# Moving a quarter of the step computation of a graph-attention layer from VectorE to GpSimd

## The chip, the cores and the metric

The kernel runs on one core of one Trainium2 chip. Time is device microseconds of that core, from one launch. Below, PE is TensorE (matmuls), DVE is VectorE, ACT is ScalarE, POOL is GpSimd and SP is SyncE. Each engine runs its own list of instructions in order; the lists are tied together only by semaphores, which an instruction raises when it completes and which another engine's list waits for.

## The reference

Two layers over a graph of 4096 nodes with 512 features, each followed by a layer norm. The change lies in the first:

```python
wh = (x @ weight).reshape(n, 8, 64)
awh_i = (wh * linear_i).sum(axis=2)
awh_j = (wh * linear_j).sum(axis=2)
e = leaky_relu(awh_i[:, None, :] + awh_j[None, :, :], negative_slope=0.2)
e = e + ((1.0 - adj) * -1e10)[:, :, None]
a = softmax(e, axis=1)
out = einsum('ijh,jhf->ihf', a, wh)
x = layernorm(x + out)
```

The second layer is an 8-head dot-product attention with the same mask, and a second residual and layer norm.

A leaky ReLU inside an exponential splits by the sign of awh_i + awh_j: on either side of zero the exponential is a product of a factor of i and a factor of j. So the kernel needs, for every pair and head, only a bit that says whether the sum is positive. That bit is the "step" below.

## The kernel before

The kernel runs in stages, one after the other: the projection (`project_gat`), tables and the transposed adjacency (`build_tables`), the first attention (`gat`, lines 442 to 687), the projections of the second layer, its attention, and the end.

In `gat` the 4096 nodes i are taken in 8 chunks of 512, and each chunk in 8 heads: 64 units. In a unit the 4096 nodes j are 32 tiles of 128, taken four at a time, a quad: 8 quads in a unit, 512 in the stage. The buffers `step`, `pos` and `neg` have 4 slots each (`RING`), one quad in a slot. For each quad n:

- ScalarE makes three of the four step tiles (line 544): a very steep sigmoid of the row `arow` (awh_i for 512 nodes, the same in all partitions) with a per-partition bias, written as fp8, 0 or 1. It waits until `pos` of quad n-4 is made.
- VectorE makes the fourth tile, number 3 (`OWN`), in `own_step`, line 562: `arow + a_j > 0`, also fp8.
- VectorE makes `pos` (`positive`, line 575), the step's bytes and-ed with the edge's bytes `strip`, over all four tiles at once as 512 words of 32 bits; then `neg` (`negative`, line 582), `pos` xor `strip`. An edge's byte is fp8 2^-6, a single bit, and the step's 1.0 has that bit set.
- TensorE uses the 16 blocks of 128x128 bytes of `pos` and of `neg` as weights and streams 130 columns of the value table through each (line 677): 32 matmuls a quad, into `acc`.

VectorE's list is written out by hand: `positive(n)`, `own_step(n + 1)`, `negative(n)`, and so on, so the step of the next quad stands between the two. After the third quad of a unit it reads the accumulators of the unit before (`evacuate`, lines 589 to 595), and after the last head of a chunk it divides, adds the residual and takes the norm's statistics, in five pieces during the quads 2 to 6 of the next unit (lines 599 to 632). `positive(n)` waits for both step makers and for the matmuls of quad n-4; `negative(n)` waits for `positive(n)` to have completed.

GpSimd's list in this stage holds only the store of the chunk's result (line 686), once per chunk. SyncE loads the tables and rows; the next row of `arow` is loaded once both step makers have finished a unit.

Of the kernel before, what the change touches and what calls it, by code (L numbers as in the profile page):

```python
# [23 lines left out]
F32 = mybir.dt.float32  # L24
# [3 lines left out]
F16 = mybir.dt.float16  # L28
F8 = mybir.dt.float8e4
U32 = mybir.dt.uint32  # L30
ALU = mybir.AluOpType
ACT = mybir.ActivationFunctionType
X = mybir.AxisListType.X
# [2 lines left out]
P = 128  # L36
N = 4096
D = 512
H = 8
F = D // H  # L40
KB = D // P
NT = N // P
CW = 512
C = N // CW
TC = CW // P
U = C * H
# [209 lines left out]
def build_tables(nc, k, adj, scr):  # L256


    with ExitStack() as ctx:
        s = Space(nc, ctx, "b")  # L260
# [88 lines left out]
        @block.vector  # L349
        def _(dve):  # L350
            link = Chain(dve, chain)
            dve.sem_inc(row_out[0], 16)
            dve.sem_inc(row_out[1], 16)
            dve.sem_inc(t_done, 2)
            dve.wait_ge(loaded, 32)
            link(nc.vector.tensor_reduce(k.top_wh[:], tops[:, 0:P], X, ALU.max))
            link(nc.vector.tensor_scalar(k.top_wh[:], k.top_wh[:], 1e-30, None, ALU.max))
            link(nc.vector.reciprocal(inv[:], k.top_wh[:]))
            m_j = tops[:, P + H:P + 2 * H].unsqueeze(1).to_broadcast([P, NT, H])

            link(nc.vector.tensor_tensor(shift[:], k.a_j[:], m_j, ALU.subtract))

            link(nc.vector.tensor_tensor(t1[:], k.a_i[:], m_j, ALU.add))
            link(nc.vector.tensor_scalar(t2[:], t1[:], SLOPE, None, ALU.mult))
            link(nc.vector.tensor_tensor(k.row_factors[:, :, :, 0], t1[:], t2[:], ALU.max))
            link(nc.vector.tensor_tensor(t1[:], t1[:], k.row_factors[:, :, :, 0], ALU.subtract))
            link(nc.vector.tensor_tensor(t2[:], t2[:], k.row_factors[:, :, :, 0], ALU.subtract))
            nc.vector.tensor_scalar(k.steep[:], k.a_j[:].rearrange("p t h -> p h t"), STEEP, None, ALU.mult).then_inc(ready, 1)
            dve.wait_ge(exped, 4)
            link(nc.vector.tensor_scalar(vf[:], vf[:], VSCALE, None, ALU.mult))  # L370
            link(nc.vector.tensor_scalar(vg[:], vf[:], inv[:, 0:1], None, ALU.mult))
            link(nc.vector.tensor_copy(vh[:], vf[:]))
            link(nc.vector.tensor_tensor(vl[:], vf[:], vh[:], ALU.subtract))
            dve.sem_inc(ready, 1)
            for i in range(0, NT // 2):
                for b in range(4):
                    g = 4 * i + b
                    dve.wait_ge(adj_in[b], 16 * (i + 1))

                    dve.wait_ge(t_done, g + 1)  # L380
                    nc.vector.tensor_scalar(none[:, b % 2], stage[:, b], EDGE, None, ALU.mult).then_inc(cast, 1)  # L381
                    dve.wait_ge(row_out[b % 2], 16 * (2 * i + b // 2 + 1))
                    nc.vector.tensor_scalar(rowm[:, b % 2], stage[:, b], BIG, -BIG, ALU.mult, ALU.add).then_inc(masked, 1)
                for b in range(2):
                    t = 2 * i + b
                    dve.wait_ge(ld[b], 16 * (i + 1))
                    for z in range(2):

                        nc.vector.tensor_tensor(prod[:, 2 * b + z, :].rearrange("p (h f) -> p h f", f=F),
                                                wh[:, b, :].rearrange("p (h f) -> p h f", f=F),  # L390
                                                vg[:, z, ds(t, 1), :].rearrange("p a h -> p h a").to_broadcast([P, H, F]),
                                                ALU.mult).then_inc(mult, 1)
                    for z in range(2):
                        dve.wait_ge(high, 2 * t + z + 1)
                        nc.vector.tensor_tensor(tab[:, b, :, z, F + 1:2 * F + 1], prod[:, 2 * b + z, :].rearrange("p (h f) -> p h f", f=F),
                                                tab[:, b, :, z, 0:F], ALU.subtract).then_inc(low, 1)
# [45 lines left out]
def gat(nc, k, x, scr):  # L442
# [6 lines left out]
    QUADS = NT // 4  # L449
    RING = 4  # L450
    OWN = 3
    with ExitStack() as ctx:
        s = Space(nc, ctx, "g")
        strip = s.sb("strip", [P, 2, NT, CW], F8)
        vals = s.sb("vals", [P, 2, NT, 2 * VG], F16)
        arow = s.sb("arow", [P, 2, CW], F32)
# [92 lines left out]
        def _(dve):  # L549
            link = Chain(dve, chain)  # L550
# [1 line left out]
            def words(ap):  # L552
                return ap.rearrange("p t i -> p (t i)").bitcast(U32)

            def own_step(n):
                u, j = n // QUADS, n % QUADS
                h, b = u % H, u % 2
                if j == 0:
                    dve.wait_ge(rows_in[b], 16 * (u // 2 + 1))
                if n >= RING:  # L560
                    dve.wait_ge(pos_made, n - RING + 1)
                nc.vector.tensor_scalar(step[:, n % RING, OWN, :], arow[:, b, :], k.a_j[:, 4 * j + OWN, h:h + 1], 0.0,
                                        ALU.add, ALU.is_gt, saturate=False).then_inc(own_stepped, 1)

            def positive(n):
                u, j = n // QUADS, n % QUADS
                c = u // H
# [63 lines left out]
                link(ins)  # L631
                nc.vector.tensor_copy(k.stats[:, c * TC:(c + 1) * TC, :], mv[:]).then_inc(y_normed, 1)

            own_step(0)
            for n in range(U * QUADS):
                u, j = n // QUADS, n % QUADS
                positive(n)
                if n + 1 < U * QUADS:
                    own_step(n + 1)
                negative(n)  # L640
                if j == 2 and u > 0:
                    evacuate(u - 1)
                if u % H == 0 and u > 0:
                    c = u // H - 1
                    if j == 2:
                        end_chunk(c)
                    if j == 3:
                        divide(c)
                    if j == 4:
                        alone(c)  # L650
                    if j == 5:
                        residual(c)
                    if j == 6:
                        norm_chunk(c)
# [25 lines left out]

        @block.gpsimd
        def _(pool):
            for c in range(C):
                pool.wait_ge(y_ready, c + 1)
                pool.sem_inc(x_used, 1)
                pool.dma_start(y_v[:, c * TC:(c + 1) * TC, :], y2[:]).then_inc(y_out, 16)
            pool.wait_ge(y_out, 16 * C)


# [686 lines left out]
def build(nc, x, adj, weight, linear_i, linear_j, Wks, Wqs, Wvs, Wo, out):  # L1376
    k, scr = Kept(), Kept()
    with ExitStack() as ctx:
        s = Space(nc, ctx, "k")

        def dram(name, shape, dt):
            return nc.dram_tensor(f"scr_{name}", shape, dt, kind="Internal").ap()

        k.identf = s.sb("identf", [P, P], F32)
        k.identb = s.sb("identb", [P, P], BF16)
        k.identh = s.sb("identh", [P, P], F16)
        k.bias_hi = s.sb("bias_hi", [P, P], F16)
        k.bias_lo = s.sb("bias_lo", [P, P], F16)
        k.offdiag = s.sb("offdiag", [P, P], BF16)
        k.ones = s.sb("ones", [P, P], F32)  # L1390
        k.mean_wh = s.sb("mean_wh", [P, D], F32)
        k.a_i = s.sb("a_i", [P, NT, H], F32)
        k.a_j = s.sb("a_j", [P, NT, H], F32)
        k.steep = s.sb("steep", [P, H, NT], F32)
        k.minus_big = s.sb("minus_big", [P, 1], F32)
        k.edgediag = s.sb("edgediag", [P, P], BF16)
        k.row_factors = s.sb("row_factors", [P, NT, H, 2], F32)
        k.top_wh = s.sb("top_wh", [P, 1], F32)
        k.stats = s.sb("stats", [P, NT, 2], F32)
        scr.a_i = dram("a_i", (H, N), F32)  # L1400
        scr.top_a = dram("top_a", (2 * H, 1), F32)
        scr.top_wh = dram("top_wh", (P, 1), F32)
        scr.wh = dram("wh", (P, NT, D), F32)
        scr.gat_v = dram("gat_v", (H, P, NT, 2 * VG), F16)
        scr.row_mask = dram("row_mask", (N, N), BF16)
        scr.edge_T = dram("edge_T", (N, N), F8)
        scr.y = dram("y", (N, D), F32)
        scr.x1 = dram("x1", (N, D), F32)
        scr.q_hi = dram("q_hi", (D, N), F16)
        scr.q_lo = dram("q_lo", (D, N), F16)  # L1410
        scr.k_hi = dram("k_hi", (D, 2 * N), F16)
        scr.k_lo = dram("k_lo", (D, 2 * N), F16)
        scr.v = dram("v", (H, P, 2 * NT, VA), F16)
        scr.offset = dram("offset", (U, CW), F16)
        scr.o = dram("o", (N, D), F32)
        make_constants(nc, k)
        project_gat(nc, k, x, weight, linear_i, linear_j, scr)
        build_tables(nc, k, adj, scr)
        gat(nc, k, x, scr)
        project_heads(nc, k, Wks, Wqs, Wvs, scr)  # L1420
        attend(nc, k, scr)
        finish(nc, k, Wo, scr, out)
# [18 lines left out]
```

## Time and profile before

| | us |
|---|---|
| median of 3 runs | 4722.33 |
| lowest, highest | 4721.46, 4722.55 |
| the profiled execution | 4729.1 |
| its span, first to last instruction | 4727.2 |
| in it, first attention | about 691 to 1802 |

The profile lists each instruction with its start and duration. An engine's duration of one instruction is longer than the distance to the next start, since VectorE begins the next one before the last results are written. Idle time is put down to whatever ended last before the waiting instruction began.

### The profile page before, as it was taken

What the parts mean: (1) busy time and instruction counts of PE and PEld (TensorE: products, weight loads), DVE (VectorE), ACT (ScalarE), POOL (GpSimd) and SP (SyncE); (2) the same over time, 40 slices, a digit from 0 to 9 for tenths busy, and PEclk for the clock granted to TensorE, in tenths of its full rate; (3) what the DMA queues carried; (4) which work ended last, traced back from release to release, by engine and by line L of the source; (5) the groups of instructions that cost most, each with busy time, mean ns of one, the idle gap of its engine ahead of it and who ended that gap; (6) DMA issues with size and microseconds to landing.
All of it is one profiled execution on the core that took longest, in us unless ns stands there. A gap on an engine that the chain in (4) does not pass through costs nothing. (4 is left out here: it accounts for less than half of the span.)

```text
span 4727.2 us, 104596 instructions
## 1 busy us (share of the span) xinstructions
PE 3947.8 (84%) x42500; PEld 2604.9 (55%) x42500; DVE 3517.3 (74%) x5963; ACT 3400.7 (72%) x4130; POOL 359.6 (8%) x559
## 2 busy tenths in 40 slices
PE   7932229888988996996599999999999999999977
PEld 4422229888888983442255555555555555555543
DVE  2255559999999994221688888888888888888834
ACT  1133349888888981111399999999999999999942
POOL 0000000000000000002002111121211112120100
PEclk9955559999999998998699999999999999999989
DMA  2289995555545444545335444353444434444223
GB/s 67 85 271 344 341 321 186 172 174 173 179 162 179 162 141 138 147 151 150 100 93 137 101 117 112 97 138 96 132 99 125 108 95 134 99 132 99 60 94 133
DMA packets 399291, 690.91 MB, mean 146 GB/s; under 512 B 79784, under 2 KB 272488, under 8 KB 361832
## 3 DMA queue, kind: packets, MB, share of 16 engines
q1 hardware_dynamic: 339040, 608.86, 43.8%
q0 software_dynamic: 16512, 58.73, 4.0%
q10 hardware_dynamic: 43280, 16.92, 1.3%
q8 instruction: 323, 5.29, 0.5%
q14 instruction: 136, 1.11, 0.1%
HBM read 532.82 MB, written 151.59 MB: 145 GB/s over the span
## 5 line engine op out<-in xcount | busy, mean ns | idle before, releaser
L1183 DVE CUSTOM_DVE_ANT_0 m_junk<-m_rough,m_rows 128x1024 bf16<-128x1024 f32 x1024 | 1253.1, 1224 | 250.1 <-PE m_rough L1050 178.2
L1132 ACT ACTIVATE m_scores<-m_strip,k_minus_big 128x1024 f32<-128x1024 fp8e4 x1024 | 1145.0, 1118 | 106.1 <-POOL m_strip L981 41.0
L677 PE MATMUL g_acc<-g_vals,g_pos 128*128 128x130 f16 x8192 | 979.9, 221 | 125.3 <-DVE g_neg L582 125.3
L544 ACT ACTIVATE g_step<-g_arow,k_steep 128x512 fp8e4<-128x512 f32 x1536 | 951.3, 709 | 137.3 <-DVE g_pos L575 132.3
L1146 ACT ACTIVATE m_whole<-m_scores 128x1024 int32<-128x1024 f32 x1024 | 1030.2, 1006 | 22.1 <-PE m_scores L1083 22.1
L677 PE MATMUL g_acc<-g_vals,g_neg 128*128 128x130 f16 x8192 | 979.7, 223 | 0.0
L1064 PE MATMUL m_acc<-m_v,m_halves 128*128 128x129 f16 (+1 forms) x16384 | 896.8, 208 | 85.4 <-ACT m_got L1109 85.4
L1064 PEld LDWEIGHTS m_acc<-m_v,m_halves 128*128 128x128 f16 x16384 | 750.7, 98 | 320.2 <-issue 284.7
L677 PEld LDWEIGHTS g_acc<-g_vals,g_pos 128*128 128x128 fp8e4 x8192 | 812.0, 99 | 141.6 <-DVE g_neg L582 101.5
L1208 DVE TENSOR_SCALAR m_halves<-m_whole 128x2048 f16<-128x2048 uint16 x1024 | 711.4, 695 | 127.0 <-ACT m_whole L1146 125.6
L677 PEld LDWEIGHTS g_acc<-g_vals,g_neg 128*128 128x128 fp8e4 x8192 | 795.9, 97 | 0.0
L1078 PE MATMUL m_scores<-m_qA,m_kA 128*128 128x512 f16 x2048 | 781.5, 382 | 10.8 <-ACT m_scores L1132 7.8
L1083 PE MATMUL m_scores<-m_qB,m_kB 65*128 65x512 f16 x2048 | 779.4, 381 | 0.0
L1050 PE MATMUL m_rough<-m_kA,m_qC 64*128 64x512 f16 x2048 | 422.9, 409 | 76.6 <-DVE m_most L1183 72.3
L1050 PEld LDWEIGHTS m_rough<-m_kA,m_qC 64*128 64x128 f16 x2048 | 115.7, 109 | 500.3 <-DVE m_most L1183 453.3
L437 PE MATMUL b_turned<-k_identb,b_none 128*128 128x128 bf16 x1024 | 115.1, 302 | 311.4 <-DVE b_none L381 300.7
L575 DVE TENSOR_TENSOR g_pos<-g_step,g_strip 128x512 uint32<-128x512 uint32 x512 | 350.4, 684 | 9.7 <-DMA g_strip<-scr_edge_T 5.7
L582 DVE TENSOR_TENSOR g_neg<-g_pos,g_strip 128x512 uint32<-128x512 uint32 x512 | 349.6, 683 | 0.0
L416 ACT CAST b_colm<-b_turned 128x2048 fp8e4<-128x2048 bf16 x64 | 119.4, 1865 | 225.0 <-DMA scr_edge_T<-b_colm 153.7
L437 PEld LDWEIGHTS b_turned<-k_identb,b_none 128*128 128x128 bf16 x1024 | 99.4, 141 | 327.6 <-DVE b_none L381 327.6
L1078 PEld LDWEIGHTS m_scores<-m_qA,m_kA 128*128 128x128 f16 x2048 | 201.2, 98 | 136.6 <-issue 11.8
L1083 PEld LDWEIGHTS m_scores<-m_qB,m_kB 65*128 65x128 f16 x2048 | 202.0, 99 | 108.4 <-issue 0.5
(146 smaller groups left out, 2990.8 us busy)
## 6 DMA issues: line engine op xcount, KB each, us to landing
g_vals<-scr_gat_v SPq DMA_DIRECT2D x128, 1040.0 KB, 5.3
m_v<-scr_v SPq DMA_DIRECT2D x64, 1032.0 KB, 7.9
b_stage<-in_adj SPq DMA_DIRECT2D x64, 1024.0 KB, 9.3
m_kA<-scr_k_hi SPq DMA_DIRECT2D x128, 512.0 KB, 6.2
scr_row_mask<-b_rowm SPq DMA_DIRECT2D x64, 512.0 KB, 8.8
m_kB<-scr_k_lo SPq DMA_DIRECT2D x64, 512.0 KB, 5.5
m_rows<-scr_row_mask POOLq DMA_DIRECT2D x64, 512.0 KB, 6.4
scr_gat_v<-b_tab SPq DMA_DIRECT2D x32, 520.0 KB, 10.1
```

The lines of the kernel that those rows point to most:

```text
L544: ins = nc.scalar.activation(step[:, n % RING, t, :], arow[:, b, :], ACT.Sigmoid, scale=STEEP, bias=k.steep[:, h, 4 * j + t:4 * j + t + 1] ...
L575: nc.vector.tensor_tensor(words(pos[:, n % RING]), words(step[:, n % RING]), words(strip[:, c % 2, 4 * j:4 * j + 4, :]), ALU.bitwise_and). ...
L582: nc.vector.tensor_tensor(words(neg[:, n % RING]), words(pos[:, n % RING]), words(strip[:, c % 2, 4 * j:4 * j + 4, :]), ALU.bitwise_xor).t ...
L677: mm = pe.matmul(acc[:, b, it, lo:hi], edges[:, n % RING, t, rows], vals[:, b, 4 * j + t, lo:hi], start=j == 0 and t == 0 and lo == 0, sto ...
L1050: mm = pe.matmul(rough[:, half, :], qC[rows_at, b, :].rearrange("k (p t) -> k p t", t=TC)[:, :, n % TC], kA[rows_at, b, at:at + CW], start ...
L1064: mm = pe.matmul(acc[:, q // 2, q % 2 * VW + at:q % 2 * VW + at + VA - skip], halves[:, st % ERING, t * CW + q * P:t * CW + (q + 1) * P, h ...
L1078: pe.matmul(to, kA[:, u % KSLOTS, m * P:(m + 1) * P], qA[:, b, :], start=False, stop=False, skip_group_check=True)
L1083: mm = pe.matmul(to, kB[0:ROWS_B, b, m * P:(m + 1) * P], qB[0:ROWS_B, b, :], start=False, stop=True, skip_group_check=True)
L1132: nc.scalar.activation(scores[:, n % 2], strip[:, 2 * st:2 * st + 2, :].rearrange("p t i -> p (t i)"), ACT.Identity, bias=k.minus_big[:, 0 ...
L1146: nc.scalar.activation(whole[:, st % 2], scores[:, st % 2], ACT.Exp, scale=0.125).then_inc(exped, 1)
L1183: nc.vector.tensor_tensor_reduce(out=junk[:, n % 2], in0=rough[:].rearrange("p a m -> p (a m)"), in1=rows[:, n % TC, n // TC * WIDE:(n // ...
L1208: nc.vector.tensor_scalar(halves[:, st % ERING].rearrange("p n z -> p (n z)"), whole[:, st % 2].bitcast(U16), HALVE, None, ALU.mult).then_ ...
```

## The change

The fourth step tile is no longer made by VectorE. `own_step` moves into GpSimd's list, where it runs ahead of VectorE by up to the ring's four slots, with the same waits: the row must have been loaded, and `pos` of quad n-4 made. VectorE's list is then `positive(n)`, `negative(n)`, `positive(n + 1)`. The GpSimd instruction is `arow > -a_j`, times 8, written as an unsigned byte: 8 is the one bit that an edge's byte has, so the and-ing gives what it gave. The negated table `minus_aj` is made once in `build_tables`. The store of a chunk's result stays on GpSimd and now stands behind the step of the ninth quad of the next chunk (and the last store at the end).

```diff
@@ build_tables, VectorE
             link(nc.vector.tensor_tensor(t2[:], t2[:], k.row_factors[:, :, :, 0], ALU.subtract))
+            link(nc.vector.tensor_scalar(k.minus_aj[:], k.a_j[:], -1.0, None, ALU.mult))
@@ gat, VectorE
-            def own_step(n):
-                u, j = n // QUADS, n % QUADS
-                h, b = u % H, u % 2
-                if j == 0:
-                    dve.wait_ge(rows_in[b], 16 * (u // 2 + 1))
-                if n >= RING:
-                    dve.wait_ge(pos_made, n - RING + 1)
-                nc.vector.tensor_scalar(step[:, n % RING, OWN, :], arow[:, b, :], k.a_j[:, 4 * j + OWN, h:h + 1], 0.0,
-                                        ALU.add, ALU.is_gt, saturate=False).then_inc(own_stepped, 1)
-
...
-            own_step(0)
             for n in range(U * QUADS):
                 u, j = n // QUADS, n % QUADS
                 positive(n)
-                if n + 1 < U * QUADS:
-                    own_step(n + 1)
                 negative(n)
@@ gat, GpSimd
-            for c in range(C):
+            def own_step(n):
+                u, j = n // QUADS, n % QUADS
+                h, b = u % H, u % 2
+                if j == 0:
+                    pool.wait_ge(rows_in[b], 16 * (u // 2 + 1))
+                if n >= RING:
+                    pool.wait_ge(pos_made, n - RING + 1)
+                nc.gpsimd.tensor_scalar(step[:, n % RING, OWN, :].bitcast(U8), arow[:, b, :], k.minus_aj[:, 4 * j + OWN, h:h + 1], 8.0,
+                                        ALU.is_gt, ALU.mult).then_inc(own_stepped, 1)
+
+            def store(c):
                 pool.wait_ge(y_ready, c + 1)
                 pool.sem_inc(x_used, 1)
                 pool.dma_start(y_v[:, c * TC:(c + 1) * TC, :], y2[:]).then_inc(y_out, 16)
+
+            for n in range(U * QUADS):
+                own_step(n)
+                if n >= H * QUADS and n % (H * QUADS) == QUADS:
+                    store(n // (H * QUADS) - 1)
+            store(C - 1)
             pool.wait_ge(y_out, 16 * C)
```

## Rows read from the trace of the kernel before

**Rows 1.** The span, from the head of the page
```profile
span 4727.2 us, 104596 instructions
```

**Rows 2.** Busy time by stretch: the attention loop, one end of a chunk
```profile
core 0: us, PE busy (x) PEld busy (x) DVE busy (x) ACT busy (x) POOL busy (x), PEclk, DMA share, GB/s
691.00:1787.00 1096.00, 985.57 (x16384) 969.37 (x16384) 1073.50 (x1930) 951.34 (x1536) 5.48 (x7) 0.97 0.52 171
1108.00:1125.00 17.00, 8.88 (x103) 8.21 (x104) 16.74 (x29) 7.53 (x12) 0.75 (x1) 0.70 0.51 169
```

**Rows 3.** Groups of instructions by line: busy us, mean ns, idle before
```profile
L544 ACT ACTIVATE g_step<-g_arow,k_steep 128x512 fp8e4<-128x512 f32 x1536 | 951.3, 709 | 137.3 <-DVE g_pos L575 132.3 <-DMA g_arow<-scr_a_i 4.9
...
L575 DVE TENSOR_TENSOR g_pos<-g_step,g_strip 128x512 uint32<-128x512 uint32 x512 | 350.4, 684 | 9.7 <-DMA g_strip<-scr_edge_T 5.7 <-PE g_acc L677 1.2 <-ACT g_step L544 0.4
L582 DVE TENSOR_TENSOR g_neg<-g_pos,g_strip 128x512 uint32<-128x512 uint32 x512 | 349.6, 683 | 0.0
L562 DVE TENSOR_SCALAR g_step<-g_arow,k_a_j 128x512 fp8e4<-128x512 f32 x512 | 245.2, 479 | 10.2 <-DMA g_arow<-scr_a_i 10.2
```

**Rows 4.** VectorE in order of time, one quad, the evacuation, next unit
```profile
1005.52 0.68 DVE L575 TENSOR_TENSOR g_pos<-g_step,g_strip 128x512 uint32<-128x512 uint32 x1
1006.12 0.48 DVE L562 TENSOR_SCALAR g_step<-g_arow,k_a_j 128x512 fp8e4<-128x512 f32 x1
1006.52 0.68 DVE L582 TENSOR_TENSOR g_neg<-g_pos,g_strip 128x512 uint32<-128x512 uint32 x1
1007.12 1.23 DVE L589 TENSOR_TENSOR g_scaled<-g_acc,k_row_factors 128x1040 f32<-128x1040 f32 x1
1008.39 0.70 DVE L593 TENSOR_TENSOR g_part<-g_scaled 128x520 f32<-128x520 f32 x1
...
1009.78 0.69 DVE L575 TENSOR_TENSOR g_pos<-g_step,g_strip 128x512 uint32<-128x512 uint32 x1
...
1025.25 0.69 DVE L575 TENSOR_TENSOR g_pos<-g_step,g_strip 128x512 uint32<-128x512 uint32 x1
```

**Rows 5.** ScalarE in order of time, the same unit
```profile
1010.51 14.81 ACT L544 ACTIVATE g_step<-g_arow,k_steep 128x512 fp8e4<-128x512 f32 x24 [0.65 <-DVE g_pos L575]
```

**Rows 6.** GpSimd in the second attention: groups, one instruction, one line's minimum/median/maximum
```profile
L999 POOL TENSOR_SCALAR m_num<-m_num 128x256 f32<-128x256 f32 x64 | 54.0, 844 | 0.0
...
L995 POOL TENSOR_SCALAR m_den<-m_got 128x4 f32<-128x4 f32 x64 | 14.3, 224 | 1792.5 <-ACT m_got L1109 1792.5
...
4543.56 0.20 POOL L998 TENSOR_TENSOR m_den<-m_den,m_got 128x4 f32<-128x4 f32 x1
...
L977 POOL TENSOR_TENSOR m_strip<-m_strip,k_offdiag x32: 402/411/946, 2246.4 to 4247.2; 128x128 fp8e4<-128x128 fp8e4 x32
```

**Rows 7.** GpSimd beside a VectorE instruction with two SBUF inputs
```profile
2581.20 0.43 DVE L1202 TENSOR_TENSOR m_o<-m_num,m_rden 128x256 f32<-128x256 f32 x1
...
2581.31 0.59 POOL L977 TENSOR_TENSOR m_strip<-m_strip,k_offdiag 128x128 fp8e4<-128x128 fp8e4 x1
...
2858.86 0.42 DVE L1202 TENSOR_TENSOR m_o<-m_num,m_rden 128x256 f32<-128x256 f32 x1
...
2859.01 0.56 POOL L977 TENSOR_TENSOR m_strip<-m_strip,k_offdiag 128x128 fp8e4<-128x128 fp8e4 x1 [5.80 <-DMA m_strip<-scr_edge_T]
```

**Rows 8.** A VectorE instruction that starts while GpSimd is at work; its usual duration
```profile
L1208 DVE TENSOR_SCALAR m_halves<-m_whole x1024: 681/690/1020, 2322.8 to 4539.9; 128x2048 f16<-128x2048 uint16 x171
...
4481.10 0.68 POOL L1001 TENSOR_TENSOR m_num<-m_num,m_got 128x256 f32<-128x256 f32 x1
...
4481.55 0.79 DVE L1208 TENSOR_SCALAR m_halves<-m_whole 128x2048 f16<-128x2048 uint16 x1 [0.96 <-ACT m_whole L1146]
```

**Rows 9.** Minimum/median/maximum of a VectorE line with one PSUM input
```profile
L1183 DVE CUSTOM_DVE_ANT_0 m_junk<-m_rough,m_rows x1024: 1203/1225/1228, 2250.9 to 4477.6; 128x1024 bf16<-128x1024 f32 x171
```

**Rows 10.** TensorE matmuls at the start of the stage, before its clock rose
```profile
699.68 0.32 PE L677 MATMUL g_acc<-g_vals,g_pos 128*128 128x130 f16 x1
699.79 0.32 PE L677 MATMUL g_acc<-g_vals,g_neg 128*128 128x130 f16 x1
```

More of the change, by code:

```diff
@@ L30 @@
 U32 = mybir.dt.uint32
+U8 = mybir.dt.uint8
 ALU = mybir.AluOpType
@@ L1394, in build @@
         k.steep = s.sb("steep", [P, H, NT], F32)
+        k.minus_aj = s.sb("minus_aj", [P, NT, H], F32)
         k.minus_big = s.sb("minus_big", [P, 1], F32)
```

## The prediction

> **What bounds the kernel now.** The change touches one stage, so I read that stage. The busy times by stretch come first: in the 1096 us of the loop VectorE is busy for 1073.5, TensorE for 985.6, ScalarE for 951.3, GpSimd for 5.5 [rows 2]. VectorE is the bound, and the other two stand close behind it. The groups by line say the same from the waiting side: `pos` and `neg` wait for almost nothing (9.7 and 0.0 us), while ScalarE idles 132.3 us for `pos` [rows 3].
>
> The order of time then gives the pace. VectorE starts `pos` at 1005.52, its own step at 1006.12, `neg` at 1006.52 and the next instruction at 1007.12 [rows 4]: 0.60 + 0.40 + 0.60 = 1.60 us a quad. An ordinary unit runs from 1009.78 to 1025.25, 15.47 us: eight quads (12.8) and the evacuation, 1007.12 to 1009.78 (2.66). 64 x 15.47 = 990; the remaining 106 us of the loop are the ends of chunks, some 13 us each. ScalarE works 14.81 of those 15.47 us and waits 0.65 [rows 5]. So even with VectorE's work gone, an ordinary unit can't fall below about 14.83.
>
> **What is removed.** 512 VectorE instructions with a distance of 0.40 us, 205 us. Not all of it comes back. `neg` reads `pos` and waits for its completion; today the own step stands in that gap. With it gone `neg` can start only when `pos` has ended, after 0.68 us, plus some 0.04 us, which is what the dependent pair of the evacuation shows (the first starts at 1007.12, takes 1.23, the second starts at 1008.39) [rows 4]. The pair costs 0.72 + 0.60 = 1.32 us a quad instead of 1.60. The saving is 0.28 us x 512 = 143 us of VectorE's time, and of this the other engines let at most about 105 through (worked out under the first rival).
>
> **What is added on GpSimd.** 512 instructions of 512 elements. The trace has no such instruction. The nearest is the one-operation scalar instruction: 224 ns for 4 elements, 844 ns for 256 [rows 6], or 2.46 ns an element; at 512 elements that is 0.224 + 508 x 0.00246 = 1.47 us. From below: the fp8 multiply of 128 elements takes 411 ns and the 4-element one 0.20 us [rows 6], 1.7 ns an element, so 1.06 us. From above: the new instruction has two operations (compare, multiply), and if the second costs as much per element as the first it takes 0.22 + 508 x 0.00492 = 2.72 us. I take 1.47, the row of the same kind of instruction, and keep both ends.
>
> By itself that fits: 1.47 us is below the 1.85 us that ScalarE needs for its three tiles. If nothing else happened, GpSimd would be hidden.
>
> **What is added between the engines.** This decides. In the second attention some GpSimd instructions meet VectorE instructions. At 2581.31 a GpSimd multiply, usually 411 ns [rows 6], takes 0.59 us; VectorE had begun an instruction with two SBUF inputs at 2581.20 and ended it at 2581.63, and GpSimd ended 0.27 us after that. At 2859.01 it happens again: 0.56 us, ending 0.28 us behind the end of the same VectorE line (2859.28) [rows 7]. GpSimd does not run slower beside such an instruction, it waits for its end. The other direction is shown for another kind: a scalar instruction of VectorE, median 690 ns, takes 0.79 us when it starts at 4481.55 while a GpSimd one of 4481.10 to 4481.78 is at work [rows 8]; its delay of 0.10 us puts its real beginning at 4481.65, 0.14 us before GpSimd's end. An instruction with one of its inputs in PSUM doesn't feel it: the maximum of the line is 1228 ns in 1024, beside a median of 1225 [rows 9].
>
> I read this as something that only one of the two can hold. GpSimd holds it from about 0.14 us after its start to 0.14 us before its end, that is for its duration less 0.28 us: H = 1.19 us for 1.47. `pos` and `neg` both have two SBUF inputs, and fill 1.2 of the 1.32 us. The own step of before was in VectorE's list and met no one.
>
> The Trainium skill, page "SBUF — State Buffer", section "SBUF: two separate sides", states the mechanism: VectorE and GpSimd share one pair of ports, and it is an exclusive lock for the whole instruction against VectorE instructions with two SBUF inputs. The rows above agree in the one direction for two SBUF inputs; no row shows GpSimd holding up such a VectorE instruction. By that rule the sum below stands; without it the first rival does.
>
> **The sum.** A quad in which the GpSimd step falls between `pos` and `neg`: `pos` 0.68 to its end, H = 1.19, then 0.60 from `neg`'s start to the next `pos`: 2.48 us, against 1.60 now, +0.88. It does not matter between which two of VectorE's instructions it falls, since there is one step for each quad and the ring of four slots keeps GpSimd from building up a lead. One step of the eight in a unit can run beside the scaled evacuation (1.23 us, one input in PSUM, no contention); that quad costs 1.32, -0.28. A unit: 7 x 0.88 - 0.28 = +5.88 us, and 64 units: +376 us. The loop goes from 1096 to about 1470 us, some 23 us a unit; ScalarE at 14.8 us a unit and TensorE at 985.6 / 64 = 15.4 are well hidden. What is behind the lock on GpSimd's list is only the chunk's store; SyncE's row load waits for both step makers at the end of a unit, and the row is for the unit after the next, so a whole unit covers it. The one added instruction in `build_tables` is below half a microsecond of VectorE in a stage that ends in transfers: nothing.
>
> The profiled execution took 4729.1 us (its span is 4727.2 [rows 1]), 6.8 above the median of the runs. 4729.1 + 376 = 5105; on the median, 4722.3 + 376 = 5098 us.
>
> The bounds of the sum: with 1.06 us for the step H is 0.78, the quad +0.46, a unit +2.97 and the time +190, 4912. With 2.72 us H is 2.44, the quad +2.12, a unit +14.6 and the time +932, 5656.
>
> One more thing can add to it. TensorE, busy for 985.6 us in 512 quads [rows 2], would work 1.92 of 2.48 us. Its granted clock fell to 0.70 in the stretch in which it was busy for 8.9 of 17 us [rows 2]; before it had risen, matmuls stood 0.11 us apart [rows 10], 32 of them 3.5 us, more than 2.48. I expect the clock to stay up, at a busy share of three quarters, and count this toward the upper end.
>
> **Rivals.**
>
> *No exclusion for these instructions (13%), faster.* Speaks for it: no row shows a VectorE instruction with two SBUF inputs being delayed by GpSimd. Against: GpSimd plainly waits for it [rows 7]. Then GpSimd at 1.47 us is hidden and ScalarE and TensorE set the pace: 64 x (15.47 - 14.83) = 41 us, and VectorE, now at 15.47 - 8 x 0.28 = 13.23 us a unit, can be four quads (7.4 us) ahead when one of seven inner chunk ends comes, and gains 7.4 + 1.6 = 9 us at each, 63. In all -104: 4618 us. It decides as soon as GpSimd's step stays below 1.85 us and does not hold up `pos`.
>
> *No exclusion, but GpSimd too slow (5%), slower.* With 2.72 us a step it is the bound itself: 512 x 2.72 = 1393 against 1096, +297, 5019 us. The break-even is at 1096 / 512 = 2.14 us a step. At this point, and only near it, lies "no change" (3%, taken from this rival and the next).
>
> *Exclusion, but a short step (6%), slightly slower.* If the step held the lock for only half a microsecond, the quad would be +0.17, a unit 7 x 0.17 - 0.28 = +0.9 and the whole +60: 4782 us. Against it stands the 844 ns for half the elements [rows 6].
>
> The Trainium skill, "GPSIMD Engine Reference", section 4.1, calls one-input elementwise work on GpSimd roughly line-rate, and section 3.1 measured 769 ns for 512 elements in a tight loop. It would give this last rival. The 844 ns row for 256 elements speaks against that rate here.
>
> **How the numbers follow.** Forecast, the exclusion with a step between 1 and 2.7 us: 76%, 5098 us. Range: from the short step, 4780, to near the upper bound, 5600; the first rival and a tail of about 5% are left out. Two measurements of this kernel can be told apart from 0.2%, some 9 us: faster 13%, within it 3%, slower 84%.
>
> **What would show it.** Right: `pos` and `neg`, 684 ns now, stretched in most quads, one of them by about 1.2 us, or idle in front of them; GpSimd's step well above 1.47 us by the profile, since its waiting counts in; ScalarE's wait for `pos` up by hundreds of us; VectorE's and GpSimd's instructions alternating. Wrong: `pos` and `neg` still at 684 ns beside a busy GpSimd (then the first rival or, with idle time before `pos` put down to GpSimd, the second). A start of `neg` less than 0.7 us behind `pos` would refute the dependent gap, and TensorE's clock at half would mean that the upper end is a matter of the clock.

## The result: 252 us slower, with GpSimd as the new bound

| | before | after |
|---|---|---|
| median, us | 4722.44 | 4974.35 |
| runs | 4721.46 to 4725.61, 4 runs | 4971.44 to 4978.14, 4 runs |
| ratio, 95% interval | | 1.0533, 1.0514 to 1.0551 |
| span of the profiled execution | 4727.2 | 4971.1 |
| ordinary unit, from the first `pos` to the next unit's | 15.47 | 20.47 |

The forecast was 5098, the range 4780 to 5600. The changed kernel's groups of instructions by line (busy us, mean ns, idle before), the lines that answer to [rows 3], with GpSimd's new one at the top:

```profile
L679 POOL TENSOR_SCALAR g_step<-g_arow,k_minus_aj 128x512 uint8<-128x512 f32 x512 | 1247.4, 2436 | 728.1 <-DMA g_arow<-scr_a_i 682.2
...
L546 ACT ACTIVATE g_step<-g_arow,k_steep 128x512 fp8e4<-128x512 f32 x1536 | 978.1, 710 | 363.8 <-DVE g_pos L567 358.7 <-DMA g_arow<-scr_a_i 3.0
...
L574 DVE TENSOR_TENSOR g_neg<-g_pos,g_strip 128x512 uint32<-128x512 uint32 x512 | 469.6, 917 | 17.6
L567 DVE TENSOR_TENSOR g_pos<-g_step,g_strip 128x512 uint32<-128x512 uint32 x512 | 372.9, 728 | 237.0 <-POOL g_step L679 205.4 <-DMA g_strip<-scr_edge_T 15.6 <-ACT g_step L546 9.2
```

The busy time of the stretch that the loop now fills, with the columns of [rows 2]:

```profile
684.00:2035.00 1351.00, 1063.67 (x16384) 1022.07 (x16384) 1094.17 (x1420) 977.64 (x1536) 1252.85 (x519) 0.93 0.43 139
```

GpSimd, the last busy figure before the clock, is at work for 1253 of 1351 us; before it was 5. `pos` idles 205 us for it, where it had waited for next to nothing, and ScalarE's wait for `pos` has gone from 132 to 359 us. A few quads in order of time, VectorE and then GpSimd (start, duration, idle before):

```profile
992.53 0.72 DVE L567 TENSOR_TENSOR g_pos<-g_step,g_strip 128x512 uint32<-128x512 uint32 x1 [0.85 <-POOL g_step L679]
993.28 0.98 DVE L574 TENSOR_TENSOR g_neg<-g_pos,g_strip 128x512 uint32<-128x512 uint32 x1
995.12 0.72 DVE L567 TENSOR_TENSOR g_pos<-g_step,g_strip 128x512 uint32<-128x512 uint32 x1 [0.86 <-POOL g_step L679]
995.87 0.98 DVE L574 TENSOR_TENSOR g_neg<-g_pos,g_strip 128x512 uint32<-128x512 uint32 x1
...
683.63 2.00 POOL L679 TENSOR_SCALAR g_step<-g_arow,k_minus_aj 128x512 uint8<-128x512 f32 x1 [682.16 <-DMA g_arow<-scr_a_i]
...
992.52 2.50 POOL L679 TENSOR_SCALAR g_step<-g_arow,k_minus_aj 128x512 uint8<-128x512 f32 x1
...
995.12 2.50 POOL L679 TENSOR_SCALAR g_step<-g_arow,k_minus_aj 128x512 uint8<-128x512 f32 x1
```

The first step of the stage, with VectorE idle, takes 2.00 us. In the steady state it takes 2.50, and one begins every 2.59 to 2.60. The completion of one step releases `pos` at the same moment as the next step begins, so each step meets a `pos`, waits for its end (993.25) and needs 1.77 us from there. `neg` takes 0.98; undisturbed, right behind `pos`, it takes 0.69 (the minimum of its line in the runs below). It is held up by 0.29 us, no more, although it lies wholly inside GpSimd's 2.5 us. That is not the long hold of the prediction, which would have kept it out until 0.14 us before GpSimd's end.

So two theories are tested, the second one formed after this trace was seen: **theory 1**, as predicted, GpSimd holds off VectorE's two-input instructions for its duration less 0.28 us; **theory 2**, it does so only while it reads its input, some 0.3 us for 512 elements, and the loss comes from GpSimd's own length, 2.0 us plus the wait for `pos`. The runs with one execution each are given beside a run of the kernel before on the same chip.

### The profile page after: what moved, and what is told of

It reads as the page before. It is cut to its first block and busy times, and to the rows that moved or that the text cites. A ratio compares the mean times of both kernels' runs of the same rounds, so it can differ in the third digit from the quotient of the medians.

```text
span 4971.1 us, 104597 instructions
## 1 busy us (share of the span) xinstructions
PE 4025.8 (81%) x42500; PEld 2656.5 (53%) x42500; DVE 3536.8 (71%) x5452; ACT 3427.8 (69%) x4130; POOL 1606.1 (32%) x1071
## 5 line engine op out<-in xcount | busy, mean ns | idle before, releaser
L679 POOL TENSOR_SCALAR g_step<-g_arow,k_minus_aj 128x512 uint8<-128x512 f32 x512 | 1247.4, 2436 | 728.1 <-DMA g_arow<-scr_a_i 682.2
L666 PE MATMUL g_acc<-g_vals,g_pos 128*128 128x130 f16 x8192 | 1049.4, 227 | 301.4 <-DVE g_neg L574 300.8
L546 ACT ACTIVATE g_step<-g_arow,k_steep 128x512 fp8e4<-128x512 f32 x1536 | 978.1, 710 | 363.8 <-DVE g_pos L567 358.7
L666 PE MATMUL g_acc<-g_vals,g_neg 128*128 128x130 f16 x8192 | 1048.0, 229 | 0.0
L666 PEld LDWEIGHTS g_acc<-g_vals,g_pos 128*128 128x128 fp8e4 x8192 | 835.9, 103 | 343.1 <-DVE g_neg L574 295.0
L666 PEld LDWEIGHTS g_acc<-g_vals,g_neg 128*128 128x128 fp8e4 x8192 | 825.0, 101 | 0.0
L1000 POOL TENSOR_SCALAR m_den<-m_got 128x4 f32<-128x4 f32 x64 | 14.4, 224 | 1791.7 <-ACT m_got L1114 1791.7
L567 DVE TENSOR_TENSOR g_pos<-g_step,g_strip 128x512 uint32<-128x512 uint32 x512 | 372.9, 728 | 237.0 <-POOL g_step L679 205.4
L574 DVE TENSOR_TENSOR g_neg<-g_pos,g_strip 128x512 uint32<-128x512 uint32 x512 | 469.6, 917 | 17.6
```

The costliest lines, as they stand in the source:

```text
L546: ins = nc.scalar.activation(step[:, n % RING, t, :], arow[:, b, :], ACT.Sigmoid, scale=STEEP, bias=k.steep[:, h, 4 * j + t:4 * j + t + 1] ...
L574: nc.vector.tensor_tensor(words(neg[:, n % RING]), words(pos[:, n % RING]), words(strip[:, c % 2, 4 * j:4 * j + 4, :]), ALU.bitwise_xor).t ...
L666: mm = pe.matmul(acc[:, b, it, lo:hi], edges[:, n % RING, t, rows], vals[:, b, 4 * j + t, lo:hi], start=j == 0 and t == 0 and lo == 0, sto ...
L679: nc.gpsimd.tensor_scalar(step[:, n % RING, OWN, :].bitcast(U8), arow[:, b, :], k.minus_aj[:, 4 * j + OWN, h:h + 1], 8.0, ALU.is_gt, ALU.m ...
```

## Experiments

**1. Nobody makes the tile.** What the removal alone is worth; GpSimd's list has the stores only.

```diff
-                dve.wait_ge(own_stepped, n + 1)
...
+            link(nc.vector.memset(step[:, :, OWN, :], 0.0))
```

> The fourth step tile is set to zero once and made by no one, so a quarter of the pairs take the negative branch; everything else is as in the changed kernel. This shows what the removal alone gives. Both theories (long hold, short hold) expect the same: pos to neg 0.72 us, the next pos 0.60 us later, VectorE no longer the bound, ScalarE and TensorE setting the pace, about 4618 us. If it comes out near 4722, the removal gave nothing even without GpSimd.

4665.6 us beside 4720.3: -54.7, half of the 104 us of the first rival. VectorE in order of time, `neg` of one quad, the next quad, and the first `pos` that waits:

```profile
1007.12 0.69 DVE L572 TENSOR_TENSOR g_neg<-g_pos,g_strip 128x512 uint32<-128x512 uint32 x1
1007.73 0.68 DVE L565 TENSOR_TENSOR g_pos<-g_step,g_strip 128x512 uint32<-128x512 uint32 x1
1008.45 0.69 DVE L572 TENSOR_TENSOR g_neg<-g_pos,g_strip 128x512 uint32<-128x512 uint32 x1
...
1014.89 0.69 DVE L565 TENSOR_TENSOR g_pos<-g_step,g_strip 128x512 uint32<-128x512 uint32 x1 [0.43 <-PE g_acc L665]
```

The dependent gap is as expected (0.72, then 0.61), and an ordinary unit takes 14.80 us. That is the floor of ScalarE and TensorE: from 1014 to 1044 us of this run both are busy for 30.0 of the 30 us. What failed is the lead of four quads at a chunk's end: that unit takes 28.3 us against 29.06 and the next 13.3 against 15.47, 3 us for each end and not 9. VectorE can't get ahead, as I read it: `pos` needs ScalarE's steps, and ScalarE makes them at the pace at which TensorE uses them up (no run separates the two). Some 55 us is thus the most that taking the fourth step off VectorE can give in this kernel.

**2. GpSimd only writes.**

```diff
-                nc.gpsimd.tensor_scalar(step[:, n % RING, OWN, :].bitcast(U8), arow[:, b, :], k.minus_aj[:, 4 * j + OWN, h:h + 1], 8.0,
-                                        ALU.is_gt, ALU.mult).then_inc(own_stepped, 1)
+                nc.gpsimd.memset(step[:, n % RING, OWN, :].bitcast(U8), 8.0).then_inc(own_stepped, 1)
```

> GpSimd writes the fourth step tile with a constant (a memset of 128x512 bytes, no read) with the same waits, so that a quarter of the pairs take the positive branch. Long hold (theory 1, as predicted: GpSimd holds what pos and neg need for its whole instruction less 0.28 us): pos or neg is stretched by roughly the memset's duration less 0.28 us. Short hold (theory 2: pos and neg collide with GpSimd only while it reads): pos and neg stay at 684 ns, and the time is that of the kernel in which nobody makes the tile, about 4618 us.

4666.0 us, the same as with nobody. The minimum/median/maximum of the lines:

```profile
L679 POOL MEMSET g_step<- x512: 524/524/552, 688.6 to 1714.5; 128x512 uint8 x171
L567 DVE TENSOR_TENSOR g_pos<-g_step,g_strip x512: 683/687/695, 694.7 to 1719.1; 128x512 uint32<-128x512 uint32 x171
L574 DVE TENSOR_TENSOR g_neg<-g_pos,g_strip x512: 691/692/694, 695.4 to 1719.8; 128x512 uint32<-128x512 uint32 x171
```

Not one of 1024 instructions is stretched beside 512 writes of 0.52 us. That alone does not speak against theory 1, because the memset usually begins just behind a `neg`:

```profile
1000.78 0.69 DVE L574 TENSOR_TENSOR g_neg<-g_pos,g_strip 128x512 uint32<-128x512 uint32 x1
...
1000.80 0.52 POOL L679 MEMSET g_step<- 128x512 uint8 x1 [1.33 <-DVE g_pos L567]
```

What speaks against it is the memset's own time. In [rows 7] GpSimd waited for the end of such an instruction; here it begins 0.02 us behind `neg`, is done 0.15 us before `neg` ends, and never takes more than 0.55 us. The two ran side by side. A GpSimd instruction that reads nothing is harmless here.

**3. Half the elements.** Columns 256 to 511 stay zero.

> GpSimd makes only 256 of the 512 columns of the fourth step tile, the other half stays zero. By the changed kernel's trace the undisturbed step takes 1.99 us and 0.22 us of it is fixed, so this one takes about 1.1 us. Theory 1 (long hold): H = 0.83, 2.1 us a quad, about 4960 us. Theory 2 (GpSimd's own duration is the bound, its hold on VectorE is short): it takes at most 1.11 + 0.09 + 0.5 = 1.70 us a quad, is no longer the bound, and the time falls to between 4640 and 4740 us. If neg is delayed by 0.15 us instead of 0.29, the hold grows with the elements that are read.

4669.7 us beside 4720.3. The step and `neg`:

```profile
L680 POOL TENSOR_SCALAR g_step<-g_arow,k_minus_aj x512: 1142/1396/3762, 685.5 to 1714.7; 128x256 uint8<-128x256 f32 x171
...
L574 DVE TENSOR_TENSOR g_neg<-g_pos,g_strip x512: 691/849/853, 692.4 to 1720.1; 128x512 uint32<-128x512 uint32 x171
```

The step is 1.14 us when undisturbed, and the delay of `neg` 849 - 691 = 0.16 us where it was 0.29: theory 2, and the delay goes with what is read. With a step this short the 55 us come nearly whole. Theory 1 (4960) is out.

**4. One operation instead of two.** `ALU.is_gt` alone.

> GpSimd's step with the comparison alone (the multiply by 8 left out), so the written byte is 1 and not the edge's bit, and the fourth tile acts as all negative. If the second operation is what makes the step 1.99 us instead of the 1.47 us that I scaled from the one-operation row, the undisturbed step falls to about 1.47 us, a quad to about 2.07, and the time to about 4740 us. If the operation costs nothing, the step stays at 1.99 and the time at 4974 us. Both theories on the hold are indifferent to it.

4745.8 us beside 4720.3. The lines:

```profile
L679 POOL TENSOR_SCALAR g_step<-g_arow,k_minus_aj x512: 1555/1717/4182, 689.9 to 1789.7; 128x512 uint8<-128x512 f32 x171
...
L574 DVE TENSOR_TENSOR g_neg<-g_pos,g_strip x512: 691/1061/1066, 696.9 to 1795.3; 128x512 uint32<-128x512 uint32 x171
```

1.56 us undisturbed, against 1.99 with both operations. My 1.47 from the one-operation row [rows 6] was right within 0.09 for one operation; the multiply adds 0.44. The total is near the 4740 that was expected, but not by the way expected, which had GpSimd as the bound at 2.07 us a quad. A quad takes 1.70 us: VectorE is the pace again, with 1.32 us and the 0.37 that `neg` now waits, against 1.60 before. So even a step of 1.56 us does not pay.

**5. GpSimd beside the kernel before.** VectorE makes every step; GpSimd makes every other one as well, into a tile that nobody reads.

> VectorE makes the fourth step tile as in the kernel before; beside it GpSimd makes the step of every other quad into a tile that nobody reads, so that GpSimd is not on the path (2.0 to 2.5 us of work in 3.2 us) and only its interference shows. Theory 1 (long hold of 1.7 us for every VectorE instruction with two SBUF inputs or two ports): 256 GpSimd steps, each delaying VectorE by up to 1.7 us, up to +435 us, pos and neg stretched to over 2 us. Theory 2 (pos and neg wait only while GpSimd reads, about 0.3 us; the scalar instruction of VectorE's own step, which by the rows of the second attention is delayed until 0.14 us before GpSimd's end, waits long): pos and neg never over about 1.1 us, the own step up to about 2.1 us, and the total in between, +75 us if VectorE's step never meets it and up to +300 us if it does each time.

4795.8 us beside 4721.7: +74. The maxima are what counts:

```profile
L567 DVE TENSOR_SCALAR g_step<-g_arow,k_a_j x512: 471/479/836, 685.8 to 1847.3; 128x512 fp8e4<-128x512 f32 x171
L580 DVE TENSOR_TENSOR g_pos<-g_step,g_strip x512: 676/684/1095, 691.9 to 1848.3; 128x512 uint32<-128x512 uint32 x171
L587 DVE TENSOR_TENSOR g_neg<-g_pos,g_strip x512: 671/681/1095, 692.9 to 1849.0; 128x512 uint32<-128x512 uint32 x171
...
L697 POOL TENSOR_SCALAR g_shadow<-g_arow,k_minus_aj x256: 1997/2659/4888, 685.8 to 1838.4; 128x512 uint8<-128x512 f32 x128
```

None of these 1536 instructions of VectorE is delayed by more than 0.41 us, beside GpSimd instructions of 2 us and more. I had left open that VectorE's own step, which has one input, would wait as long as theory 1 says; it too is held up, but by 0.36 at most. GpSimd fares worse: up to 4.89 us for 2.00 of work.

**6. Two inputs.** GpSimd adds two inputs of 512 elements and nobody reads the sum; the fourth tile stays zero.

```diff
+                nc.gpsimd.tensor_tensor(junk[:, n % RING, :], arow[:, b, :], arow[:, b, :], ALU.add).then_inc(own_stepped, 1)
```

> In place of the step GpSimd adds two inputs of 512 elements each (the row with itself) and writes the sum where nobody reads it; the fourth step tile stays zero. By the rows of the second attention this takes about 1.27 us (203 ns for 4 elements, 730 for 256), less than the step, but it reads twice as much. Hold in proportion to what is read (0.16 us for 256 elements, 0.29 to 0.37 for 512 were seen): pos or neg delayed by 0.6 to 0.75 us a quad, VectorE about 2.0 us a quad, about 4930 us. A fixed hold of 0.3 us: 1.62 us a quad, about 4730. The hold of the prediction, duration less 0.28, 0.99 us: 2.3 us a quad, about 5080.

4943.5 us beside 4719.9. The lines, and a meeting in order of time:

```profile
L568 DVE TENSOR_TENSOR g_pos<-g_step,g_strip x512: 683/1527/1530, 688.6 to 1995.4; 128x512 uint32<-128x512 uint32 x171
...
L683 POOL TENSOR_TENSOR g_junk<-g_arow x512: 1038/1544/1549, 682.5 to 1990.0; 128x512 f32<-128x512 f32 x171
...
1002.30 0.69 DVE L575 TENSOR_TENSOR g_neg<-g_pos,g_strip 128x512 uint32<-128x512 uint32 x1
1002.91 1.53 DVE L568 TENSOR_TENSOR g_pos<-g_step,g_strip 128x512 uint32<-128x512 uint32 x1
...
1002.34 1.54 POOL L683 TENSOR_TENSOR g_junk<-g_arow 128x512 f32<-128x512 f32 x1 [0.63 <-DVE g_pos L568]
```

An instruction half as long as the step (1.04 against 1.99 us) costs almost the same, because `pos` waits 1527 - 683 = 0.84 us. Usual delays at three sizes: 0.16 us for 256 elements read, 0.29 to 0.41 for 512, 0.84 for 1024. The time is within 14 us of what the proportional hold gave, with a delay somewhat above the 0.6 to 0.75 us expected.

This run does not separate the theories, though. The length that I assumed, 1.27 us, was too long; with the measured 1.04 us theory 1 gives a hold of 0.76 us, and that is what the meeting shows. GpSimd waits for `neg` to end (1002.99), and the delay of 0.84 puts the real beginning of `pos` at 1003.75, 0.76 us later and 0.13 before GpSimd's end (1003.88). So "duration less 0.28" holds for a GpSimd instruction with two inputs, here as in [rows 8] (512 elements in 0.68 us, a hold of 0.40 by the rule). It is the step, with one input and two operations, whose hold is a small part of its duration. That the hold goes by the elements read is shown for the step alone (256 against 512). The third size differs in the operation, the number of inputs and the bytes written too, and fits.

**7 and 8. The step where its read meets no one.** VectorE keeps seven of eight (six of eight) steps; GpSimd makes the fifth quad's (and the sixth's), and starts when `neg` of the third is made. `SHARED` is (4,) in the one and (4, 5) in the other; the lines are VectorE's and then GpSimd's. The chunk's store stands one quad earlier.

```diff
+                if n + 1 < U * QUADS and (n + 1) % QUADS not in SHARED:
+                    own_step(n + 1)
...
+                if j == SHARED[0]:
+                    pool.wait_ge(neg_made, QUADS * u + 3)
```

> GpSimd makes the step of one quad in eight only (the fifth of a unit), and begins it when neg of the third is made, so that its read falls into the evacuation's first instruction (1.23 us, one input in PSUM), where the short hold meets no one; VectorE makes the other seven. Theory 2 (the hold is short and only while GpSimd reads): VectorE saves 0.28 us a unit, 64 x 0.28 = 18 us, about 4704 us, with pos, neg and the evacuation at their old durations. If the hold lasts for the whole instruction: part and num of the evacuation delayed by about 0.5 us, no gain or a loss of some 15 us.

> As the kernel before it in this call, with two steps in a unit (the fifth and the sixth quad) on GpSimd, one behind the other. The second starts 2.08 us after the first and its read meets the evacuation's last two small instructions or the next pos. If it costs VectorE nothing: 0.56 us a unit, about 4687 us. If it delays pos by the full 0.3 us: no more than the other, about 4704 us.

With one: 4704.2 us (4702.3 to 4709.9, 6 runs) beside 4719.9, ratio 0.9966 (0.9954 to 0.9978). With two: 4713.0 us (11 runs), 0.9986 (0.9977 to 0.9995). GpSimd and VectorE with one:

```profile
1012.54 2.00 POOL L699 TENSOR_SCALAR g_step<-g_arow,k_minus_aj 128x512 uint8<-128x512 f32 x1 [13.21 <-DVE g_neg L590]
...
1012.30 1.24 DVE L597 TENSOR_TENSOR g_scaled<-g_acc,k_row_factors 128x1040 f32<-128x1040 f32 x1
1013.57 0.70 DVE L601 TENSOR_TENSOR g_part<-g_scaled 128x520 f32<-128x520 f32 x1
...
1014.97 0.69 DVE L583 TENSOR_TENSOR g_pos<-g_step,g_strip 128x512 uint32<-128x512 uint32 x1
1015.70 0.69 DVE L590 TENSOR_TENSOR g_neg<-g_pos,g_strip 128x512 uint32<-128x512 uint32 x1
```

The step runs at its undisturbed 2.00 us, beside `part` too, which has two SBUF inputs and keeps its 0.70 us: 1.03 us after its start GpSimd no longer holds what `part` needs. Units take 15.20 us in place of 15.47, 0.27 us where the arithmetic gave 0.28, and the total falls by 15.7 us where 18 were expected. This version is 0.34% faster than the kernel before, and so the fastest of those that compute the result. With two, the second step begins 2.1 us behind the first, when VectorE has come to the evacuation's last instruction, 128x4 elements with two SBUF inputs, which took 0.17 us before:

```profile
1015.44 0.56 DVE L603 TENSOR_TENSOR g_den<-g_part 128x4 f32<-128x4 f32 x1
```

It waits 0.39 us, which is more than the 0.28 us saved: units of 15.33 us, and the total between the other two. A single hold takes back the gain of a step. Both totals expected for it, 4687 and 4704 us, were too low: what is held up is the small instruction, and by more than 0.3 us.

## Why the prediction was right, and where it was not

**The direction and its reason: half right.** Slower because the step and VectorE's two-input instructions exclude each other was the forecast. They do, in both directions: `neg` is stretched in most quads, and the step by 0.50 us. But VectorE's list, stretched in this way, is not what sets the pace. The Trainium skill, "SBUF — State Buffer", "SBUF: two separate sides", states that the lock is held for the whole instruction and that, against VectorE's instructions with two SBUF inputs, it needs a GpSimd instruction that reads SBUF. The first the measurements do not bear out for a GpSimd step with one input (0.16 us of 1.14, 0.29 to 0.44 of 1.99); for the add with two inputs they nearly do (0.76 of 1.04). The second they bear out (experiment 2).

**The hold: the step that failed.** "For its duration less 0.28 us" was carried from a GpSimd instruction with two inputs, 512 elements in 0.68 us, to a step that reads as many in 1.99 us. The usual delay is 0.29 us, in the changed kernel 0.44 at most, where a hold of 1.19 was forecast. For the two-input instruction the rule is right (experiment 6). The row had two readings, an offset from the end or an amount read, and I took the first without a second row to separate them.

**GpSimd's length: mis-sized.** 1.47 was assumed, 1.06 to 2.72 held open, 1.99 measured. The one-operation row held for one operation (1.56); the second adds 0.44.

**The sum came out near by two errors of opposite sign.** Forecast: VectorE's list bound, 2.48 us a quad. Measured: GpSimd's list bound, 2.00 + 0.50 (waiting for `pos`) + 0.09 (to the next start) = 2.59 in the steady state, 20.47 / 8 = 2.56 with the evacuation in it. Over the whole: an ordinary unit +5.0 us; a chunk's end only +1.3 (30.4 against 29.06), because there VectorE is slow enough to hide GpSimd, and the unit after it +0.5: 6 x 5.0 + 1.8 = 31.8 us a chunk, 254 in eight, against 252 between the medians and 244 between the spans (the first chunk has no end of another in it, and the first `pos` of the stage stands at 697.5 us in the one trace and at 689.7 in the other). The second rival had the right bound (a step beyond 2.14 us a quad) for the wrong reason: alone the step would fit in 2.08; it is the collision with `pos` that puts it over. That 4974 lies in the stated range is to that extent luck. Experiment 4 is close to the case that the prediction computed, a step of 1.56 us where 1.47 was assumed, and took 4745.8 us, below the range. Of the prediction's own terms, `pos` to its end, the hold and 0.60 add up to 2.47, not 2.48; that changes nothing.

**The other points.** The dependent gap was right to 0.01 us. The first rival's 104 us was 55: its term for the chunk's end, 9 us, was 3. The clock did not decide anything: the granted clock was 0.93 in the loop against 0.97, and `pos` idled 4 us in all for TensorE. What was to show the prediction right named `pos` or `neg` stretched by 1.2 us; the trace answered 0.29, with idle time put down to GpSimd, which I had listed under "wrong".

## What to carry to other kernels

Before moving work to GpSimd, ask for its length there (a second operation is not free: 0.44 us for 512 elements) and for how much it reads: what it reads is time taken from VectorE's instructions with two SBUF inputs, here mostly 0.16, 0.29 to 0.41 and 0.84 us for 256, 512 and 1024 elements, and such an instruction can hold GpSimd up in return. A move that relieves VectorE by 0.28 us and reads for 0.37 is a loss even if GpSimd is fast enough. It can gain where the read is placed beside an instruction with an input in PSUM: place it by a wait, and take only as many as fit there.

## What the runs showed of the hardware that I had not expected

- The hold of a one-input GpSimd instruction is short against its duration: in experiment 5 a 2.0 us step delayed none of 1536 VectorE instructions by more than 0.41 us, and in experiment 7 one placed at an evacuation's start ran beside a two-input instruction at full speed. For a two-input add it is nearly the whole, 0.76 of 1.04 us.
- GpSimd's memset of 0.52 us and VectorE's instruction with two SBUF inputs ran side by side, at their undisturbed times both.
- Where VectorE's instructions follow one another without a gap, GpSimd can be kept out for long: 4.89 us for a step of 2.00, in experiment 5.
- A completion that starts work on two engines at one moment makes them collide each time. The step's completion starts both `pos` and the next step; in 244 of 512 quads `pos` waited for GpSimd's step, and the usual step lost 0.50 us to the `pos` that its forerunner had released.
